# Graph layer with residual and layer norm: the last 512 nodes handled differently

## The reference

```
support = x @ weight
y = x + (1 - t) * support + t * (adj @ support)
out = (y - mean(y)) / sqrt(var(y) + 1e-5)        # per node, over the 256 features
```

## Time and profile before

| | |
|---|---|
| median of 3 runs | 395.97 us |
| the profiled execution | 395.5 us |
| its span in the trace | 393.7 us |
| busy share of the span | PE 96%, DVE 58%, ACT 37%, POOL 12% |
| mean granted TensorE clock | 0.994 |

### The profile page before, as it was taken

How to read it: one execution, slowest core, us unless ns; L and a number is a source line. 1 busy time by engine, 2 the same in 40 slices (tenths; PEclk the granted TensorE clock), 3 DMA queues, 4 the chain that set the end, 5 groups by cost and what they waited for, 6 DMA issues and landing times.

```text
span 393.7 us, 4192 instructions
## 1 busy us (share of the span) xinstructions
PE 379.0 (96%) x1737; PEld 315.7 (80%) x1737; DVE 227.7 (58%) x277; ACT 143.8 (37%) x101; POOL 46.9 (12%) x21
## 2 busy tenths in 40 slices
PE   5999999999999999999999999999999999999972
PEld 3778888888888888888888888888888888888862
DVE  2499967634775446933666445763378345684025
ACT  4776342432433335233243235233342323423010
POOL 3599420010000100001000100001000010000000
PEclk9999999999999999999999999999999999999997
DMA  7999996565665664566645657547555666610001
GB/s 255 422 422 390 338 382 218 214 229 168 245 216 167 261 247 170 208 234 234 219 189 195 237 203 267 212 162 268 187 197 203 217 224 252 210 57 2 0 1 53
DMA packets 17810, 84.41 MB, mean 214 GB/s; under 512 B 1792, under 2 KB 6144, under 8 KB 9728
## 3 DMA queue, kind: packets, MB, share of 16 engines
q1 hardware_dynamic: 17520, 83.89, 58.0%
q10 hardware_dynamic: 272, 0.26, 0.2%
HBM read 79.95 MB, written 4.19 MB: 214 GB/s over the span
## 4 chain that ended last, share of the span: by engine, by line
PE 90%; DVE 4%; DMA 3%; SPq 1%; issue 1%; ACT 1%; DVEq 0%
PE agg L324 28%; PE agg L326 28%; PE agg L325 28%; DMA a_raw<-in_adjT 3%; DVE a_lo L236 2%; PE out_ps L365 2%; PE out_ps L367 2%; PE out_ps L366 2%; DVE w_lo L303 1%; ACT a_hi L174 0%; SPq L136 0%; DVE x_raw L264 0%; SPq L107 0%; DVE x_raw L289 0%; DVE z_lo L255 0%
## 5 line engine op out<-in xcount | busy, mean ns | idle before, releaser
L236 DVE TENSOR_TENSOR a_lo<-a_raw,a_hi 128x2048 fp32r<-128x2048 f32 x63 | 155.0, 2467 | 129.0 <-ACT a_hi L174 129.0
L324 PE MATMUL agg<-a_hi,x_hi 128*128 128x512 f32 x512 | 200.6, 392 | 4.1 <-DVE a_lo L297 3.3
L325 PE MATMUL agg<-a_lo,x_hi 128*128 128x512 f32 x512 | 200.3, 391 | 0.0
L326 PE MATMUL agg<-a_hi,x_lo 128*128 128x512 f32 x512 | 200.0, 391 | 0.0
L174 ACT ACTIVATE a_hi<-a_raw 128x2048 fp32r<-128x2048 f32 x63 | 120.7, 1915 | 146.4 <-PE agg L326 138.9
L324 PEld LDWEIGHTS agg<-a_hi,x_hi 128*128 128x128 f32 x512 | 96.7, 189 | 25.5 <-issue 3.9
L326 PEld LDWEIGHTS agg<-a_hi,x_lo 128*128 128x128 f32 x512 | 96.7, 189 | 20.2
L325 PEld LDWEIGHTS agg<-a_lo,x_hi 128*128 128x128 f32 x512 | 96.7, 189 | 19.9
L220 POOL TENSOR_TENSOR xt<-xt,omt_col 128x1024 f32<-128x1024 f32 x8 | 18.6, 2324 | 261.6 <-DMA xt<-in_xT 261.6
L214 POOL TENSOR_TENSOR x_lo<-x_raw,x_hi 128x1024 fp32r<-128x1024 f32 x8 | 27.5, 3457 | 11.1 <-ACT x_hi L166 11.1
L181 ACT ACTIVATE z_hi<-z 128x512 fp32r<-128x512 f32 x16 | 10.1, 633 | 45.3 <-DVE z L249 45.3
(11 more groups left out here) (22 smaller groups left out, 49.0 us busy)
## 6 DMA issues: line engine op xcount, KB each, us to landing
a_raw<-in_adjT SPq DMA_DIRECT2D x63, 1024.0 KB, 4.8
x_raw<-in_x SPq DMA_DIRECT2D x8, 512.0 KB, 6.4
xt<-in_xT SPq DMA_DIRECT2D x8, 512.0 KB, 5.7
rows<-in_x SPq DMA_DIRECT2D x8, 512.0 KB, 5.6
out<-x_raw SPq DMA_DIRECT2D x7, 512.0 KB, 3.0
a_raw<-in_adjT SPq DMA_DIRECT2D x4, 256.0 KB, 6.0
out<-x_raw SPq DMA_DIRECT2D x4, 128.0 KB, 1.8
w_raw<-in_W ACTq DMA_DIRECT2D x1, 256.0 KB, 4.4
```

The costliest lines, as they stand in the source:

```text
L236: nc.vector.tensor_tensor(a_lo[:, slot], a_raw[:, slot], a_hi[:, slot].bitcast(f32), ALU.subtract).then_inc(a_lo_ready[slot], 1)
L324: nc.tensor.matmul(bank, x_hi[:, j, cols], a_hi[:, slot, b], start=first, stop=False)
L325: nc.tensor.matmul(bank, x_hi[:, j, cols], a_lo[:, slot, b], start=False, stop=False)
L326: return nc.tensor.matmul(bank, x_lo[:, j, cols], a_hi[:, slot, b], start=False, stop=last)
```

## The change

Only the last chunk is changed, with some preparation on POOL. There
- DVE makes z and z_lo of half 0 before it turns to half 1; z, z_hi and z_lo of half 1 are made in two pieces of 256 nodes;
- PE's `project_last` runs the 12 matmuls of half 0 for all four tiles, then adds the residual in PSUM by an identity matmul with x_hi and one with x_lo for each tile, then the 12 of half 1, in the order of the two pieces. The identity (128x128, fp32r) is made by POOL after `x_low`, with two memsets and an affine_select;
- the residual add on DVE and the last load of `rows` are left out; bn_stats and the normalisation read PSUM;
- the Sqrt takes eps as its bias, reading the variance directly; the Newton step has one instruction fewer; a new `shift` = -mean * rstd is computed for ACT;
- DVE normalises tiles 0 and 1, stored by SP, and ACT tiles 2 and 3, stored from ACT's own queue.

```diff
@@ sync
-                    if g == 5:
+                    if g == 5 and c + 1 < CHUNKS:
                         load_rows(c)
-            for i in range(TILES):
-                c = CHUNKS - 1
+            c = CHUNKS - 1
+            for i in range(2):
                 sp.wait_ge(normed_ready, c * TILES + i + 1)
                 sp.dma_start(out[...], normed(c)[:, i]).then_inc(stored[c % 2], 16)
+            sp.wait_ge(act_stored, 16 * 2)
@@ scalar
-            z_high(CHUNKS - 1)
-            root(CHUNKS - 1)
+            c = CHUNKS - 1
+            act.wait_ge(prod_ready[TILES - 1], c)
+            act.wait_ge(z_ready[0], c + 1)
+            nc.scalar.activation(z_hi[:, 0], z[:, 0], ACT.Copy).then_inc(z_hi_ready[0], 1)
+            for h in range(2):
+                cols = slice(h * (WIDE // 2), (h + 1) * (WIDE // 2))
+                act.wait_ge(z_ready[1], c + h + 1)
+                nc.scalar.activation(z_hi[:, 1, cols], z[:, 1, cols], ACT.Copy).then_inc(z_hi_ready[1], 1)
+            act.wait_ge(eps_ready, 1)
+            act.wait_ge(mean_var_ready, (c + 1) * TILES)
+            nc.scalar.activation(std[:, :], mean_var[:, :, 1], ACT.Sqrt, bias=eps_col[:, :]).then_inc(std_ready, 1)
+            act.wait_ge(shift_ready, 1)
+            for i in range(2, TILES):
+                nc.scalar.activation(normed(c)[:, i], out_ps[i][:, 0:feats], ACT.Identity, bias=shift[:, i:i + 1],
+                                     scale=rstd[:, i:i + 1]).then_inc(act_normed_ready, 1)
+            for i in range(2, TILES):
+                act.wait_ge(act_normed_ready, i - 1)
+                act.dma_start(out[...], normed(c)[:, i]).then_inc(act_stored, 16)
@@ gpsimd, behind x_low
+            nc.gpsimd.memset(eps_col[:, :], EPS).then_inc(eps_ready, 1)
+            nc.gpsimd.memset(z[:, 0, 0:P], 1.0).then_inc(ones_ready, 1)
+            pool.wait_ge(ones_ready, 1)
+            nc.gpsimd.affine_select(ident[:, :], z[:, 0, 0:P], pattern=[[-1, P]], base=0, channel_multiplier=1,
+                                    compare_op=ALU.is_equal, fill=0.0).then_inc(ident_ready, 1)
@@ vector
-            make_z(CHUNKS - 1)
-            layernorm(CHUNKS - 1)
+            nc.vector.scalar_tensor_tensor(z[:, 0], agg[c % 2][0][:, :], t_col[:, :], xt[:, c % 2, 0],
+                                           ALU.mult, ALU.add).then_inc(z_ready[0], 1)
+            dve.wait_ge(z_hi_ready[0], c + 1)
+            nc.vector.tensor_tensor(z_lo[:, 0], z[:, 0], z_hi[:, 0].bitcast(f32), ALU.subtract).then_inc(z_lo_ready[0], 1)
+            dve.wait_ge(a_used[RING - 1], turn(c, GROUPS - 1) + 1)
+            halves = [slice(h * (WIDE // 2), (h + 1) * (WIDE // 2)) for h in range(2)]
+            for h in range(2):
+                nc.vector.scalar_tensor_tensor(z[:, 1, halves[h]], agg[c % 2][1][:, halves[h]], t_col[:, :],
+                                               xt[:, c % 2, 1, halves[h]], ALU.mult, ALU.add).then_inc(z_ready[1], 1)
+            for h in range(2):
+                dve.wait_ge(z_hi_ready[1], c + h + 1)
+                nc.vector.tensor_tensor(z_lo[:, 1, halves[h]], z[:, 1, halves[h]], z_hi[:, 1, halves[h]].bitcast(f32),
+                                        ALU.subtract).then_inc(z_lo_ready[1], 1)
+            for i in range(TILES):
+                dve.wait_ge(prod_ready[i], c + 1)
+                nc.vector.bn_stats(stats[:, i], out_ps[i][:, 0:feats]).then_inc(stats_ready, 1)
...
+            nc.vector.reciprocal(rstd0[:, :], std[:, :]).then_inc(rstd0_ready, 1)
+            nc.vector.scalar_tensor_tensor(newton_s[:, :], rstd0[:, :], -0.5, rstd0[:, :], ALU.mult, ALU.mult
+            nc.vector.tensor_tensor(newton_q[:, :], newton_s[:, :], var_eps[:, :], ALU.mult)
+            nc.vector.scalar_tensor_tensor(rstd[:, :], newton_q[:, :], 1.5, rstd0[:, :], ALU.add, ALU.mult
+            nc.vector.scalar_tensor_tensor(shift[:, :], mean_var[:, :, 0], -1.0, rstd[:, :], ALU.mult, ALU.mult
...
+            for i in range(2):
+                nc.vector.tensor_scalar(normed(c)[:, i], out_ps[i][:, 0:feats], mean_var[:, i, 0:1], rstd[:, i:i + 1],
+                                        ALU.subtract, ALU.mult).then_inc(normed_ready, 1)
@@ tensor
+            def project_last():
+                c = CHUNKS - 1
+                pe.wait_ge(z_lo_ready[0], c + 1)
+                for i in range(TILES):
+                    ...
+                    pe.wait_ge(y_ready[i], c)
+                    nc.tensor.matmul(dst, z_hi[:, 0, cols], w_hi[:, 0], start=True, stop=False)
+                    nc.tensor.matmul(dst, z_hi[:, 0, cols], w_lo[:, 0], start=False, stop=False)
+                    nc.tensor.matmul(dst, z_lo[:, 0, cols], w_hi[:, 0], start=False, stop=False)
+                pe.wait_ge(ident_ready, 1)
+                for i in range(TILES):
+                    dst = out_ps[i][:, 0:feats]
+                    nc.tensor.matmul(dst, ident[:, :], x_hi[:, c * TILES + i], start=False, stop=False)
+                    nc.tensor.matmul(dst, ident[:, :], x_lo[:, c * TILES + i], start=False, stop=False)
+                for h in range(2):
+                    pe.wait_ge(z_hi_ready[1], c + h + 1)
+                    for i in (2 * h, 2 * h + 1):
+                        cols = slice(i * P, (i + 1) * P)
+                        nc.tensor.matmul(out_ps[i][:, 0:feats], z_hi[:, 1, cols], w_hi[:, 1], start=False, stop=False)
+                        nc.tensor.matmul(out_ps[i][:, 0:feats], z_hi[:, 1, cols], w_lo[:, 1], start=False, stop=False)
+                    pe.wait_ge(z_lo_ready[1], c + h + 1)
+                    for i in (2 * h, 2 * h + 1):
+                        cols = slice(i * P, (i + 1) * P)
+                        nc.tensor.matmul(out_ps[i][:, 0:feats], z_lo[:, 1, cols], w_hi[:, 1], start=False, stop=True
+                                         ).then_inc(prod_ready[i], 1)
-            project(CHUNKS - 1)
+            project_last()
```

More of the change, by code:

```diff
@@ L63, in gnn_layernorm_kernel @@
         rstd = sb("rstd", [P, TILES])
+        shift = sb("shift", [P, TILES])
+        eps_col = sb("eps_col", [P, 1])
+        ident = sb("ident", [P, P], f32r)
         def y_tile(i):
@@ L94, in gnn_layernorm_kernel @@
         rstd_ready, normed_ready = sem("rstd_ready"), sem("normed_ready")
+        eps_ready, ones_ready, ident_ready = sem("eps_ready"), sem("ones_ready"), sem("ident_ready")
+        shift_ready, act_normed_ready = sem("shift_ready"), sem("act_normed_ready")
+        act_stored = sem("act_stored")
         stored = sems("stored", 2)
@@ L159, in _ @@
             sp.wait_ge(stored[0], 16 * (CHUNKS // 2))
-            sp.wait_ge(stored[1], 16 * (CHUNKS // 2 - 1 + TILES))
+            sp.wait_ge(stored[1], 16 * (CHUNKS // 2 - 1 + 2))
+            sp.wait_ge(act_stored, 16 * 2)
         @block.scalar
@@ L206, in _ @@
                         root(c - 1)
-            z_high(CHUNKS - 1)
-            root(CHUNKS - 1)
+            c = CHUNKS - 1
[15 more added lines that the diff above has]
+                act.wait_ge(act_normed_ready, i - 1)
+                act.dma_start(out[c * WIDE + i * P:c * WIDE + (i + 1) * P], normed(c)[:, i]).then_inc(act_stored, 16)
         @block.gpsimd
@@ L315, in _ @@
                         layernorm(c - 1)
-            make_z(CHUNKS - 1)
-            layernorm(CHUNKS - 1)
+            c = CHUNKS - 1
+            dve.wait_ge(xt_scaled, c + 1)
+            dve.wait_ge(agg0_ready, c + 1)
+            dve.wait_ge(prod_ready[TILES - 1], c)
+            nc.vector.scalar_tensor_tensor(z[:, 0], agg[c % 2][0][:, :], t_col[:, :], xt[:, c % 2, 0],
+                                           ALU.mult, ALU.add).then_inc(z_ready[0], 1)
+            dve.wait_ge(z_hi_ready[0], c + 1)
@@ new lines, in _ @@
+            for h in range(2):
[6 more added lines that the diff above has]
+            for i in range(TILES):
+                dve.wait_ge(stats_ready, c * TILES + i + 1)
+                nc.vector.bn_aggr(mean_var[:, i], stats[:, i]).then_inc(mean_var_ready, 1)
@@ new lines, in _ @@
+            dve.wait_ge(mean_var_ready, (c + 1) * TILES)
+            nc.vector.tensor_scalar(var_eps[:, :], mean_var[:, :, 1], EPS, None, ALU.add).then_inc(var_eps_ready, 1)
+            dve.wait_ge(std_ready, c + 1)
+            nc.vector.reciprocal(rstd0[:, :], std[:, :]).then_inc(rstd0_ready, 1)
+            dve.wait_ge(rstd0_ready, c + 1)
+            nc.vector.scalar_tensor_tensor(newton_s[:, :], rstd0[:, :], -0.5, rstd0[:, :], ALU.mult, ALU.mult
+                                           ).then_inc(newton_s_ready, 1)
@@ new lines, in _ @@
+            dve.wait_ge(newton_s_ready, c + 1)
+            dve.wait_ge(var_eps_ready, c + 1)
+            nc.vector.tensor_tensor(newton_q[:, :], newton_s[:, :], var_eps[:, :], ALU.mult).then_inc(newton_q_ready, 1)
+            dve.wait_ge(newton_q_ready, c + 1)
+            nc.vector.scalar_tensor_tensor(rstd[:, :], newton_q[:, :], 1.5, rstd0[:, :], ALU.add, ALU.mult
```

(8 more changed lines are left out.)

## The result

The changed kernel takes 393.6 us (median of 4 runs, 393.4 to 393.61) beside 396.33 us for the one before in the same session (395.9 to 396.87): a ratio of 0.9931, 95% interval 0.9914 to 0.9947. A second session gave 0.9937 (0.9918 to 0.9955). The profiled execution has a span of 391.9 us.

A forecast was written before the change was run, and what follows sets the result against it. The body was taken as an uninterrupted PE matmul stream, so only the end counted: first store 2.16 us earlier plus 0.2 us from the stores gave 2.4 us, forecasting 393.6 us, 8-in-10 range 392.8 to 395.0.

The forecast's parts named there:

- PE's start: Last chunk's projection: z_lo of half 0 made earlier lets PE start 2.44 us earlier, with no gap.
- 20 matmuls of cover: Half 0's 12 projection matmuls plus 8 identity ones, 2.4 us, during which half 1's z pieces get ready.
- The split at nothing: Making half 1's z, z_hi and z_lo in two pieces gains nothing, since the undivided form would also be in time.
- Statistics from PSUM: DVE's bn_stats reading PSUM costs 0 extra (bounds -0.02 to 0.06 us each); aggregates come 1.97 us earlier.
- The chain to rstd: Aggregates to first normalisation: 1.85 us becomes 1.65; root and Newton step save 0.20 each, shift adds 0.20.
- The stores: Last four stores on two queues: bound by transfer, 2.9 us from first issue to last landing against 3.1, gaining 0.2 us.
- Hidden: Dropped rows load and POOL's identity preparation cost nothing on the path; affine_select taken as under 1 us.
- The sum: Whole end of the kernel: 2.16 + 0.2 = 2.4 us gained, giving 393.6 us median and a span of 391.3.
- rival in which the stores overlap fully: Last stores: the two queues are not held by the transfer, last landing 3.0 us earlier, 393.0 us; chance 0.10.
- rivals of ScalarE's slow queue: ScalarE's stores land late: after 4.4 us, 395.6 us, chance 0.08; or after 6.4 us, 397.6 us, chance 0.04.
- rival 2: End: PSUM statistics, a ScalarE table reload and ScalarE's activations are dear; gain only 1.4 us, 394.6 us; chance 0.16.

The follow-up runs named there:

- e2: Changed kernel with half 1's z, z_hi and z_lo made in one piece of 512 nodes instead of two: 393.65 us, ratio 0.9919 to the kernel before.
- e6: Changed kernel with the root taken from var_eps without a bias from memory, as before the change: 393.9 us (one run).
- e4: Changed kernel with all four last stores issued by SP, ScalarE still normalising tiles 2 and 3: 394.18 us, ratio 0.9946 to the kernel before.
- e7: Changed kernel with each of the last four stores writing only 128 of 256 columns, so output is incomplete: 392.93 us (one run).
- e3_dve_add: Changed kernel with DVE adding the residual from rows again instead of the eight identity matmuls: 394.35 us, ratio 0.9936 to the kernel before.
- e5_dve_norm: Changed kernel with DVE normalising all four tiles from PSUM, no shift, SP issuing all stores: 393.73 us, ratio 0.9931 to the kernel before.
- c1_before_again: The kernel before the change, unaltered, profiled once more: 396.88 us (one run).

## Why the prediction was right

- **PE's start** 2.44 us earlier, 20 matmuls of cover, +0.96 us for the identity: measured 2.67 - 0.23 = 2.44, no gap, 8 x 0.117 = 0.93. Right.
- **The split at nothing**: right, by e2.
- **Statistics from PSUM** at the price of SBUF: 0.423 us against 0.428. The aggregates came 2.08 us earlier instead of 1.97: DVE started 0.04 us behind tile 0's last matmul instead of the 0.10 I took from the row of before, and that matmul came 0.04 us sooner by its slightly shorter steps.
- **The chain to rstd** came out at 387.97 - 386.30 = 1.67 us for 1.65 forecast, but by two errors that cancel, which is luck. Leaving out var_eps ahead of the root saves 0.05 instead of 0.20 us, by e6. The shift costs 0.08 us instead of 0.20, since DVE's normalisation starts that soon behind it (387.97 - 387.89). The Sqrt with a bias from memory is 0.09 us longer than the one without. These 0.09 us are what the rule of the Trainium skill quoted there gives; I had weighed it and left it out of the sum. The trace of the changed kernel also has ScalarE's normalisations at 0.559 us, against the 0.42 I took; by the rule, added to my 0.42, it would have been 0.61. No run separates what this cost at the end. DVE's normalisation from PSUM, at 0.537 instead of 0.41 us, moved the first store by 0.12 us. First store 2.13 us earlier instead of 2.16: the 0.11 gained at the statistics paid for it.
- **The stores**: bound by transfer, 2.9 us assumed from first issue to last landing; the DMA share of 1.04 and 340 GB/s, e4 and e7 bear it out. From the first store to the end it is 3.36 us instead of 3.62, so this part gained 0.26 us for 0.2 forecast, and not 3. The rival in which the stores overlap fully is out.
- **Hidden**: affine_select took 2.05 us and the three POOL instructions pushed the scaling of xt from 40.44 to 42.76:

```profile
40.74 2.05 POOL L253 TENSOR_SCALAR_AFFINE_SELECT ident<-z 128x128 fp32r<-128x128 f32 x1
42.76 3.93 POOL L243 TENSOR_TENSOR xt<-xt,omt_col 128x1024 f32<-128x1024 f32 x1
```

  More than the 1 us I took, but free: from PE's last wait in the body, near 29 us, to the last aggregation matmul all fourteen traces have 352.04 to 352.09 us.
- **The sum**: 2.39 us in the tail for 2.4 forecast. That the median, 393.6 us, fits exactly is luck. For a profiled execution I forecast 393.1 us and a span of 391.3; measured are 393.61 and 391.9, because the last aggregation matmul came 0.59 us later than in the trace of before (381.51 against 380.92). I had added 0.47 us for the distance of the median of before from its profiled execution, and this made up for it. Nor did I see that the time of before has an upper level behind PE's wait; one of the three runs shown, 396.87, was on it. Against the mean of the lower level the change gains 2.2 us (0.6%), against the upper 3.4 us, and how much a session shows depends on how many runs fell on each.

The rivals of ScalarE's slow queue are out: its stores landed after 2.0 to 2.3 us. Of the dear forms of rival 2, only ScalarE's normalisations came near: the statistics cost no more, and the only ACT_TABLE_LOAD of the changed kernel is the one at 1.29 us.

## What to carry to other kernels

Price a wait by what its follower can do with the time, not by its length: the order alone closed PE's 2.28 us down to 0.80 and gave 0.33 us, since the first tile was hardly ready sooner; with half 1 in pieces as well the aggregates came 1.15 us earlier, and only with DVE's adds gone too 2.08 us. At the end of a kernel, let the last results come evenly spaced rather than in groups, so that only one tile's work lies behind the last matmul. And close even short waits of TensorE ahead of its last matmuls: beside the wait itself they can, as far as the traces here tell, cost the clock in some executions and not in others, so look for two levels in the times.

## What the runs showed of the hardware

A per-partition normalisation (TENSOR_SCALAR, 256 columns) on DVE takes 0.41 us from SBUF and 0.535 to 0.537 from PSUM, whether ScalarE works beside it or not, while bn_stats costs the same from both. From e3_dve_add (SBUF), then from e5_dve_norm (PSUM, no ScalarE beside it):

```profile
L390 DVE TENSOR_SCALAR x_raw<-x_raw,mean_var,rstd 128x256 f32<-128x256 f32 x2 | 0.7, 408 | 0.0
```

```profile
L375 DVE TENSOR_SCALAR x_raw<-out_ps,mean_var,rstd 128x256 f32<-128x256 f32 x4 | 1.9, 535 | 0.0
```

ScalarE's normalisation takes 0.591 us from SBUF and 0.559 from PSUM.

One thing stays open: PE's last wait near 29 us ends at 28.8 to 29.0 in the three traces without the change's other parts and at 29.1 to 29.7 in the eleven with them, before any changed instruction has run. Its ranges nearly touch, and no run separates chance from, say, where code and tensors lie. But it is less than the first two traces suggest. The changed kernel run again has its last aggregation matmul at 381.10, within 0.1 us of c1_before_again's 381.00. And if the tails are as in the traces, the timed runs' spans give its place: for the kernel before on the lower level, ten spans of 393.7 to 394.3 us less 12.78 are 380.9 to 381.5, mean 381.2; for the changed one, eight spans of 391.5 to 392.0 less 10.39 are 381.1 to 381.6, mean 381.4. What the change may cost in the body is thus about 0.2 us, which would make up the difference between the 2.39 us of the tail and the 2.2 us of the times.
